# A graph convolution's message fetch by mask products on TensorE and one maximum on VectorE, and a bank per tile in the next block's opening

## The chip, the cores and the metric

One core of a Trainium2 chip runs the whole program. The metric is device time in microseconds (us) of one execution; lower is better. Engines are named as in the profile: PE (TensorE; PEld are its weight loads), DVE (VectorE), ACT (ScalarE), POOL (GpSimd), SP (SyncE, which only issues transfers here). "POOLq" and the like are an engine's sequencer.

## The reference

Four layers on 6250 nodes of 512 features follow each other; the change touches the first, a two-layer graph convolution over 100,000 edges (`src`, `dst`, sorted by `dst`) with hidden width H = 8:

```python
def _gcn_conv(x, W, b, src, dst, norm):
    h = x @ W
    msg = h[src] * norm[:, None]
    return jax.ops.segment_sum(msg, dst, num_segments=N) + b
h = _gcn_conv(x, W1, b1, src, dst, norm)        # 512 -> 8
h = relu(layernorm(h) * gamma + beta)
out = relu(_gcn_conv(h, W2, b2, src, dst, norm)) * size_factors   # 8 -> 512
x = x + out                                      # x here is the input of the layer norm before
x = x + ffn_bitlinear(_layernorm(x))             # weights quantised in groups of 128, 1408 wide
x = x + graph_mean(_layernorm(x)) ; x = x + switch_moe(_layernorm(x))
```

## The kernel before

The program has four blocks with a barrier between them. The nodes lie in NT = 49 tiles of 128, the edges in 784 chunks of 128.

**Block A** (until 188 us) makes the hidden features `hid` of all nodes, the degrees and the edge lists, and stores the source ids' low parts as `lo_rows` in device memory.

**Block B** (190 to 813 us) is the first convolution's sum over edges. Each edge needs the 8 values of its source node: `msg_b`, one chunk at a time. There are two ways to fetch a chunk. POOL gathers it by an indirect DMA (`gather_units`, L122; 464 chunks). Or PE, DVE and ACT fetch it without a gather: M = 80 groups g of 4 chunks. SP loads the low ids of the group (`low`), ACT turns them into masks (`far`, L1093, then `los`, L1099, two each: 128 low ids of the even and of the odd tiles of a pair), PE multiplies the masks with the node values kept in SBUF (`parts`; three bf16 parts, two halves: 6 products for each chunk, `products`, L1131), which leaves in PSUM for each edge the 8 values of each of HT = 25 tile pairs, and DVE picks the right pair: four multiplications by a compare with the edge's tile number (`masked`, L927) and one sum over 25 (L935), into `picked`. Beside this loop the same engines quantise the feed-forward weights: 22 "wide" pieces (DVE L882 to L899, PE transposes L1140, ACT copy L1078, DVE `wide_rest` L906), one every second group, and 4 "down" pieces (DVE L882 to L913, PE L1150, ACT L1086, DVE L919). `piece_at` says at which group a piece stands, and `back` how many groups later its next step comes. `split_picked` (L947 to L953) splits what was picked in three bf16 parts, in four groups of five.

After the loop come some 50 small steps (L991 to L1022), and then the 49 tiles: for each, DVE copies the messages of 20 chunks (`mstage`, L183) and builds a one-hot of 128x2560 (L184), PE multiplies them (L210) and DVE reduces the result (L1028). Two buffers alternate (`onehot`, `onehot_b`). A tile waits until its chunks have come (`msg_ready`), those of POOL included. In these inputs every tile takes one unit of 20 chunks and begins some 16 chunks after the one before.

**Block C** (from 814 us) is the second convolution and the feed-forward layer. Its messages `msg_c` are fetched in the same two ways, MC = 8 groups (32 chunks) by products and 752 by POOL. Its opening is serial: the products, then tiles 0 to 3 (`own_rows` L1562, the unit of `build_unit` L163 to L173, PE L219 to L229, ACT `aggT` L1452), then the layer of each (PE L1368, ACT L1462, DVE L1572), statistics, norm and transposes (PE L1375, ACT L1480, DVE L1607), and only then the first feed-forward products (L1386). All tiles of the opening use one PSUM bank, `pB`. The order is written in `groups`: `first` and `ahead` are tables of steps by place.

**Block D** (from some 2100 us) is the last two layers; the change doesn't touch it.

Of the kernel before, what the change touches and what calls it, by code (L numbers as in the profile page):

```python
# [4 lines left out]
F32 = mybir.dt.float32  # L5
# [37 lines left out]
M = 80  # L43
MB = 5
LR = 4
HT = -(-NT // 2)
assert 4 * M * P <= E and 4 * M % V == 0 and M % MB == 0 and 4 * MB == U
MC = 8
# [130 lines left out]
def build(nc, dve, b, c0, t, firsts, dstT, ids, onehot, msg, mstage, ready, msg_ready):  # L179
# [8 lines left out]
def build_units_beside(nc, dve, t, units_done, free, ended, ranges, firsts, dstT, ids, onehot, msg, mstage, ready, used, msg_ready):  # L188

    c0, units = tile_range(dve, ranges, t)  # L190
    with dve.Fori(0, units) as b:
        n = built(nc, dve, units_done)
        dve.wait_ge(used, nc.s_assert_within(dve.snap(free), 1, NT * (CU + 1) + 1, skip_runtime_bounds_check_because="units of the tiles, plus one"))
        build(nc, dve, b, c0, t, firsts, dstT, ids, onehot, msg, mstage, ready, msg_ready)
# [6 lines left out]
def sum_rows(nc, pe, t, units_done, ranges, mstage, identb, zerob, acc, onehot, ready, used):  # L201
# [3 lines left out]
    with pe.Fori(0, units):  # L205
# [3 lines left out]
        for k in range(U):  # L209
            last = nc.tensor.matmul(acc, onehot[:, k, :], mstage[:, k, :], start=False, stop=False)  # L210
# [25 lines left out]
def groups(loop, part):  # L236
# [56 lines left out]
    for steps in (first, ahead):  # L293
        for place in sorted(steps):
            run(steps[place], 0, 0)
# [34 lines left out]
def program(nc, x, src, dst, node_vec, W1, b1, gamma, beta, W2, b2, w_gate, w_up, w_down,  # L330
            alpha, Wg, bg, switch_w, switch_b, expert_w, expert_b, out):
    with ExitStack() as whole:
# [18 lines left out]
        def dram(name, shape, dt):  # L351
# [6 lines left out]
        lo_rows = dram("lo_rows", (C, P), BF16)  # L358
        lasts = dram("lasts", (1, NT), F32)
# [24 lines left out]
        early_hi = sb(convs, "early_hi", [P, 4 * MC], F32)  # L384
# [6 lines left out]
            "span var std degs degs_std span_ps spanr row_ps ranges lows numbers pool hid1 stored ".split())}  # L391
        x_in = [[sem(f"a_x_in{j}_{k}") for k in range(G)] for j in range(2)]
        with ExitStack() as ctx:
# [6 lines left out]
            low_b = sb(ctx, "low_b", [EP, EB * P], BF16)  # L400
            hi_f = sb(ctx, "hi_f", [EP, EB, P], F32)
# [43 lines left out]
            def _(sp):  # L445
# [29 lines left out]
                sp.wait_ge(s["ext_out"], 48)  # L475
# [27 lines left out]
            def _(dve):  # L503
# [84 lines left out]
                def low_ids():  # L588
                    own.step(nc.vector.tensor_single_scalar(hi_i[:], src_em[:], 2 * P - 1, ALU.bitwise_and))
                    own.step(nc.vector.tensor_copy(low_b[:], hi_i[:]))  # L590
                    dve.sem_inc(s["lows"], 1)

# [165 lines left out]
            "tail picked d_wq d_ps d_hi d_lo d_out ohs prod masked reduced parts far".split())}  # L758
        w_in = [sem(f"b_w_in{j}") for j in range(2)]
        wd_in = sem("b_wd_in")  # L760
        lo_in = [sem(f"b_lo_in{j}") for j in range(LR)]
        landed = [sem(f"b_landed{h}") for h in range(2)]
        with ExitStack() as ctx:
# [43 lines left out]
            def piece_at(g):  # L807
                if g < 4 * FB:
                    return ("wide", g // 2) if g % 2 == 0 else None
# [1745 lines left out]
```

## Time and profile before

| | us |
|---|---|
| runs of the kernel | 3475.45, 3487.32, 3489.5 |
| median | 3487.32 |
| span of the profiled execution (its own time; nothing else is listed with it) | 3485.4 |
| busy in it: PE, DVE, ACT, POOL | 2719.8, 2119.6, 1256.3, 2093.5 |

In the timelines below a row is one instruction or several alike, with start, duration, engine, line, operation, what is written and read, and in brackets how long the engine sat idle before it and what released it. Without brackets the row began as soon as the engine was free. "<-issue" is idle time in which the engine waited for no semaphore that the profile shows: its sequencer was at work.

### The profile page before, as it was taken

To read this page: it belongs to the slowest core of one execution; us is meant where nothing else is said; L and a number is where in the kernel's file an instruction comes from. 1 tells how busy PE (TensorE), PEld (TensorE's weight loads), DVE (VectorE), ACT (ScalarE), POOL (GpSimd) and SP (SyncE) were. 2 spreads that over 40 slices of the span, in tenths; PEclk is the share of its full clock that TensorE was granted. 3 is DMA by queue.
4 is the path that set the end of the run, shared out by engine and by line. 5 is a ranking of instruction groups with operands and counts; after the bars stand their busy time and mean duration, and the time that the engine had idled before them with its cause. 6 is when DMAs were issued, how large, how long until landed. Compare 5 with 4: busy or idle time off the path is not lost. (4 is left out here: it accounts for less than half of the span.)

```text
span 3485.4 us, 58362 instructions
## 1 busy us (share of the span) xinstructions
PE 2719.8 (78%) x15905; PEld 1951.7 (56%) x15906; DVE 2119.6 (61%) x4040; ACT 1256.3 (36%) x2029; POOL 2093.5 (60%) x2157
## 2 busy tenths in 40 slices
PE   6955557222799999999989995778787878878899
PEld 6945546122577777777777774333343433335687
DVE  8778888986466666666666655333444344443676
ACT  2444457002345444444444554001121212214444
POOL 0067777775777777777760002777777777772454
PEclk9667779556799999999999997999999999998899
DMA  3122233002133333333332324777777777775564
GB/s 100 61 60 48 48 81 80 5 5 54 29 105 98 98 100 94 95 95 103 91 104 94 104 100 157 215 227 232 231 240 232 244 235 246 236 240 170 175 213 128
DMA packets 237234, 459.23 MB, mean 132 GB/s; under 512 B 80060, under 2 KB 102828, under 8 KB 236994
## 3 DMA queue, kind: packets, MB, share of 16 engines
q0 software_dynamic: 111360, 235.84, 25.3%
q1 hardware_dynamic: 125634, 220.46, 19.1%
q8 instruction: 118, 1.93, 0.2%
q14 instruction: 122, 1.00, 0.1%
HBM read 389.41 MB, written 73.25 MB: 133 GB/s over the span
## 5 line engine op out<-in xcount | busy, mean ns | idle before, releaser
L122 POOL DMA_INDIRECT msg_c<-hid_rows,srcT x752 | 762.8, 1014 | 240.1 <-issue 224.9
L1868 POOL DMA_INDIRECT rows<-xn_rows,srcT x784 | 742.9, 948 | 268.6 <-issue 241.6
L2019 PE MATMUL pV<-rows,oh 128*128 x2240 | 554.4, 395 | 143.3 <-DVE oh L2332 59.0
L122 POOL DMA_INDIRECT msg_b<-hid_rows,srcT x464 | 453.5, 977 | 148.3 <-issue 135.8
L1386 PE MATMUL pGc<-xT,wgu_hi 128*128 128x384 f32 (+1 forms) x1848 | 476.7, 380 | 38.7 <-ACT gate_sum L1486 21.7
L2019 PEld LDWEIGHTS pV<-rows,oh 128*128 x2240 | 223.6, 100 | 459.9 <-issue 287.1
L1417 PE MATMUL acc<-wd,hT 128*128 128x512 f32 x1617 | 405.7, 398 | 18.0 <-DVE hT L1630 18.0
L1386 PEld LDWEIGHTS pGc<-xT,wgu_hi 128*128 128x128 f32 x1848 | 340.0, 192 | 105.8 <-issue 60.6
L1417 PEld LDWEIGHTS acc<-wd,hT 128*128 128x128 f32 x1617 | 302.9, 189 | 89.8 <-issue 29.7
L2332 DVE SCALAR_TENSOR_TENSOR oh<-ids,bases,dstT 128x896 f32 x160 | 184.2, 1151 | 225.0 <-issue 161.6
L2320 DVE TENSOR_TENSOR agg<-agg,pV x161 | 110.2, 685 | 321.6 <-PE pV L2019 320.7
L1131 PE MATMUL pG<-parts,los 128*128 128x200 bf16 x1920 | 222.4, 286 | 37.4 <-ACT los L1099 19.2
L1131 PEld LDWEIGHTS pG<-parts,los 128*128 128x128 bf16 x1920 | 202.1, 114 | 56.4 <-ACT los L1099 27.6
L2170 ACT ACTIVATE wg<-agg,invdeg 128x512 f32 (+1 forms) x49 | 35.3, 721 | 544.9 <-DVEq L111 544.9
L1851 POOL IOTA bases<- 128x49 f32 x1 | 0.2, 188 | 330.6 <-POOLq L349 330.6
L2047 PE MATMUL pW<-wgT,aT 128*128 128x512 f32 x392 | 183.2, 611 | 13.0 <-DVEq L2355 12.7
L2114 PE MATMUL pY<-weT,erT 128*128 128x512 f32 (+1 forms) x768 | 193.1, 400 | 0.0
L1620 DVE SCALAR_TENSOR_TENSOR up_sum<-pU,wscale,up_sum 128x512 f32<-128x512 f32 (+1 forms) x154 | 105.1, 682 | 127.7 <-ACT up_sum L1492 123.7
L1492 ACT ACTIVATE up_sum<-pGc,wscale 128x512 f32<-128x512 f32 (+1 forms) x154 | 97.7, 634 | 215.3 <-PE pGc L1386 215.2
L1614 DVE SCALAR_TENSOR_TENSOR gate_sum<-pGc,wscale,gate_sum 128x512 f32<-128x512 f32 (+1 forms) x154 | 105.4, 685 | 111.1 <-PE pGc L1386 76.3
L1386 PE MATMUL pGc<-xT,wgu_lo 128*128 128x512 f32 (+1 forms) x462 | 171.0, 370 | 0.0
L1386 PE MATMUL pU<-xT,wgu_hi 128*128 128x512 f32 (+1 forms) x616 | 165.2, 390 | 6.2 <-DVE up_sum L1620 6.2
(402 smaller groups left out, 4663.6 us busy)
## 6 DMA issues: line engine op xcount, KB each, us to landing
wd<-wd_rows SPq DMA_DIRECT2D x154, 512.0 KB
we<-in_L_ffn_expert_w SPq DMA_DIRECT2D x16, 1024.0 KB, 8.7
x_rows<-xr SPq DMA_DIRECT2D x49, 256.0 KB, 3.4
xn_rows<-pair SPq DMA_DIRECT2D x49, 256.0 KB, 2.0
rows<-xn_rows,srcT POOLq DMA_INDIRECT x784
res<-x_rows SPq DMA_DIRECT2D x49, 256.0 KB, 3.9
x_rows<-agg SPq DMA_DIRECT2D x49, 256.0 KB, 4.2
xt<-in_x SPq DMA_DIRECT2D x48, 256.0 KB, 2.8
```

The costliest lines, as they stand in the source:

```text
L122: nc.gpsimd.indirect_dma_start(msg[:, c, :], None, table, bass.IndirectOffsetOnAxis(ap=srcT[:, c:c + 1], axis=0)).then_inc(landed[u % 2], 16)
L1131: last = nc.tensor.matmul(into, los[:, g % 2, b, k * P:(k + 1) * P], parts[:, j, b].rearrange("p f h -> p (f h)"), start=(b == 0 and j == ...
L1386: last = nc.tensor.matmul(ps[:, 0:n], w, v, start=(m == 0), stop=(m == len(terms) - 1))
L1417: last = nc.tensor.matmul(acc4[j][:], h, wd[:, slot, w, :], start=(f == 0 and m == 0), stop=(f == FB - 1 and m == 2))
L1614: nc.vector.scalar_tensor_tensor(gate_sum[:, 0:n], pG[1][:, 0:n], wscale[:, f, 1:2], gate_sum[:, 0:n], ALU.mult, ALU.add).then_inc(s["gate ...
L1620: nc.vector.scalar_tensor_tensor(up_sum[:, 0:n], pU[0][:, 0:n], wscale[:, FB + f, 0:1], up_sum[:, 0:n], ALU.mult, ALU.add).then_inc(s["up_ ...
L1868: nc.gpsimd.indirect_dma_start(rows[:, u % RING, c, :], None, xn2_rows, bass.IndirectOffsetOnAxis(ap=srcT[:, u * Q + c:u * Q + c + 1], axi ...
L2019: last = nc.tensor.matmul(pV[:, ds(to, 1), :].rearrange("p a d -> p (a d)"), oh[:, ds(to, 1), c, :].rearrange("p a d -> p (a d)"), rows[:, ...
L2047: nc.tensor.matmul(pW[:], aT[:, k % 2, c, :], wgT[:, c, :], start=(c == 0), stop=False)
L2114: last = nc.tensor.matmul(pY[f % 2][0:n, :], erT[:, f % 2, j, c, 0:n], weT[:, e % 2, k, c, :], start=(j, k, c) == terms[0], stop=(j, k, c) ...
L2320: nc.vector.tensor_tensor(at, at, pV[:, ds((v + 1) % 2, 1), :].rearrange("p a b -> p (a b)"), ALU.add).then_inc(s["added"], 1)
L2332: nc.vector.scalar_tensor_tensor(oh[:, ds(v % 2, 1)].rearrange("p a q n -> p (a q) n"), bc(ids.unsqueeze(1), (P, Q, P)), bases[:, ds(tile, ...
```

## The change

In block B the number of groups goes from 80 to 110 (440 chunks), POOL gathers the other 344. A group's work is another. DVE makes the mask of the odd tiles by one compare (`odd`), ACT makes only the even one (`far`, `los`) and a new mask `beside` from the high ids: |tile pair of the edge - own partition| on 25 partitions. For each chunk PE first multiplies `beside` with `outside`, which holds -2^122 where the row is the column's tile pair, and adds the six products as before: a wrong pair gets a value near -2^122 or lower, the right one its own. DVE then takes one maximum over 25, straight from PSUM (`pick`). Three groups are under way instead of two (AHEAD), six loads instead of four (LB). A wide piece stands at every third group, a down piece at every tenth. Block A makes the high ids (`high_b`) and stores them (`hi_rows`). The tiles of block B build the one-hot in pairs of bf16 from small numbers (`rel`, `pairs`), as block C did already. `parts` is made by six copies with dense output instead of three with a strided one, and the eight steps for `hiT` are gone.

In block C the opening has MC = 10 groups in the new form, all low ids are loaded ahead of `node_vec` and `x`, tiles 0 to 3 have a bank each and an order of their own (`opening`).

```diff
-M = 80
+M = 110
+MW = 3
+MD = 10
+AHEAD = 3
-MC = 8
+MC = 10
@@ build (block B's tiles)
+    nc.vector.tensor_scalar(rel, dstT[:, at], firsts[:, ds(t, 1)], None, ALU.subtract).then_inc(related, 1)
     nc.vector.tensor_copy(mstage[:], msg[:, at, :])
-    nc.vector.scalar_tensor_tensor(onehot[:], bc(ids.unsqueeze(1), (P, U, P)), firsts[:, ds(t, 1)],
-                                   bc(dstT[:, at].unsqueeze(2), (P, U, P)), ALU.add, ALU.is_equal).then_inc(ready, 1)
+    dve.wait_ge(related, n + 1)
+    full = (P, U // 2, P, 2)
+    nc.vector.tensor_tensor(pairs, bc(numbers.unsqueeze(1), full), bc(rel.rearrange("p (g j) -> p g j", j=2).unsqueeze(2), full),
+                            ALU.is_equal).then_inc(ready, 1)
@@ groups
-    for steps in (first, ahead):
-        for place in sorted(steps):
-            run(steps[place], 0, 0)
+    opening = [(part.prepare, 0), (part.prepare, 1), (part.prepare, 2), (part.prepare, 3),
+               (part.build, 0), (part.sums, 0), (part.build, 1), (part.layer1, 0), (part.sums, 1), (part.build, 2), (part.layer1, 1),
+               (part.sums, 2), (part.build, 3), (part.layer1, 2), (part.sums, 3), (part.layer1, 3),
+               (part.stats, None), (part.scale, None), (part.norm, 0), (part.norm, 1),
+               (part.turn, 0), (part.norm, 2), (part.turn, 1), (part.norm, 3), (part.turn, 2), (part.turn, 3)]
+    run(opening, 0, 0)
@@ block B, DVE
-                def select(g):
+                def odd(g):
+                    dve.wait_ge(lo_in[g % LB], (g // LB + 1) * 16)
+                    if g >= AHEAD:
+                        dve.wait_ge(s["prod"], g - AHEAD + 1)
+                    nc.vector.tensor_scalar(los[:, g % AHEAD, 1, :], lo8[:, g % LB, :], lanes[:, 3:4], None, ALU.is_equal).then_inc(s["odds"], 1)
+
+                def pick(g):
                     dve.wait_ge(s["prod"], g + 1)
...
+                    nc.vector.tensor_reduce(picked[:, g // MB % 2, 4 * (g % MB):4 * (g % MB) + 4, :].rearrange("p (b c) f -> p b (c f)", b=2),
+                                            pG[g % AHEAD][:, :, 0:2 * H * HT].rearrange("p b (c h) -> p b c h", h=HT),
+                                            AX, ALU.max).then_inc(s["reduced"], 1)
@@ block B, ACT
+                    nc.scalar.activation(far[:], lo8[:, g % LB, :], ACT.Abs, bias=lanes[:, 0:1]).then_inc(s["far"], 1)
...
+                    nc.scalar.activation(beside[:, g % AHEAD, :], hi8[:, g % LB, :], ACT.Abs, bias=lanes[0:HT, 0:1]).then_inc(s["besides"], 1)
                     act.wait_ge(s["far"], g + 1)
...
+                    nc.scalar.activation(los[:, g % AHEAD, 0, :], far[:], ACT.Relu, bias=lanes[:, 2:3], scale=-1.0).then_inc(s["evens"], 1)
@@ block B, PE
+                    pe.wait_ge(s["besides"], g + 1)
+                    pe.wait_ge(s["evens"], g + 1)
+                    pe.wait_ge(s["odds"], g + 1)
+                    if g >= AHEAD:
+                        pe.wait_ge(s["reduced"], g - AHEAD + 1)
                     for k in range(4):
...
+                        nc.tensor.matmul(into, beside[:, g % AHEAD, k * P:(k + 1) * P], outside[:].rearrange("p f h -> p (f h)"), start=True, stop=False)
```

Three places show how the order of instructions changes. First DVE in block B's loop, at the first wide piece, before:

```order
L927 SCALAR_TENSOR_TENSOR masked<-iota,hiT,pG 128x200 x4
L935 TENSOR_REDUCE picked<-masked 128x32
L906 TENSOR_TENSOR wgu_lo<-pW,wgu_hi 128x256
L927 SCALAR_TENSOR_TENSOR masked<-iota,hiT,pG 128x200 x4
L935 TENSOR_REDUCE picked<-masked 128x32
L882 TENSOR_REDUCE sc<-wraw 128x4
```

and in the changed kernel, between two wide pieces:

```order
L969 TENSOR_REDUCE picked<-pG 128x32
L963 TENSOR_SCALAR los<-lo,lanes 128x512
L969 TENSOR_REDUCE picked<-pG 128x32
L963 TENSOR_SCALAR los<-lo,lanes 128x512
L943 TENSOR_TENSOR wgu_lo<-pW,wgu_hi 128x256
L969 TENSOR_REDUCE picked<-pG 128x32
L963 TENSOR_SCALAR los<-lo,lanes 128x512
L919 TENSOR_REDUCE sc<-wraw 128x4
```

Five DVE instructions a group became two, and `wide_rest` comes after the second group behind its piece instead of after the first. Second, DVE at one tile of block B (ISA, TENSOR_LOAD, REGISTER_ALU and branches are the sequencer's own instructions), before:

```order
L144 TENSOR_LOAD ranges
L144 ISA x2
L191 UNCONDITIONAL_BRANCH
L191 ISA
L181 ISA
L183 ISA
L183 COPY mstage_b<-msg_b 128x480
L184 ISA
L184 SCALAR_TENSOR_TENSOR onehot_b<-ids_b,firsts,dstT 128x2560
L195 ISA
L191 COMPARE_AND_BRANCH
```

and now:

```order
L151 TENSOR_LOAD ranges
L151 ISA x2
L201 UNCONDITIONAL_BRANCH
L201 ISA
L188 ISA
L190 ISA
L190 TENSOR_SCALAR rels<-dstT,firsts 128x20
L191 ISA
L191 COPY mstage_b<-msg_b 128x480
L192 REGISTER_ALU
L194 TENSOR_TENSOR onehot_b<-numbers_b,rels 128x2560
L205 ISA
```

The sequencer's work is all there still, with one instruction more on DVE. Third, PE behind block C's first tile; before, the next thing was tile 1's sums in the same bank:

```order
L229 MATMUL pB<-identb,zerob 32x128 x4
L144 TENSOR_LOAD ranges
L144 ISA x2
L219 MATMUL pB<-identb,own_rows 32x128
L219 MATMUL pB<-identb,zerob 32x128 x3
```

now the tile's layer comes first, and the next tile's sums go to another bank:

```order
L239 MATMUL pB<-identb,zerob 32x128 x4
L1439 MATMUL accs<-w2b,aggT 128x512
L151 TENSOR_LOAD ranges
L151 ISA x2
L229 MATMUL pU<-identb,own_rows 32x128
L229 MATMUL pU<-identb,zerob 32x128 x3
```

## Rows read from the trace of the kernel before

**Rows 1.** The gathers of blocks B and C, by line: duration min/median/max, first and last start

```profile
L122 POOL DMA_INDIRECT msg_c<-hid_rows,srcT x752: 938/944/2239, 815.1 to 1816.8; - x188
L122 POOL DMA_INDIRECT msg_b<-hid_rows,srcT x464: 938/944/1736, 191.2 to 791.8; - x155
```

**Rows 2.** Timeline of DVE at the end of block B

```profile
795.25 0.28 DVE L183 COPY mstage<-msg_b 128x480 bf16 x1 [7.70 <-POOLq L872]
...
799.16 0.18 DVE L1028 TENSOR_REDUCE agg<-pW 128x8 f32<-128x24 f32 x1 [0.75 <-PE pW L212]
```

**Rows 3.** Timeline of DVE in block B's loop, a wide piece and a down piece

```profile
204.22 0.99 DVE L935 TENSOR_REDUCE picked<-masked 128x32 f32<-128x800 f32 x1
205.12 0.68 DVE L882 TENSOR_REDUCE sc<-wraw 128x4 f32<-128x512 f32 x1
...
209.75 1.42 DVE L927 SCALAR_TENSOR_TENSOR masked<-iota,hiT,pG 128x200 f32<-128x200 f32 x4
...
492.68 1.61 DVE L882 TENSOR_REDUCE sc<-wdraw 128x11 f32<-128x1408 f32 x1
...
501.66 1.42 DVE L927 SCALAR_TENSOR_TENSOR masked<-iota,hiT,pG 128x200 f32<-128x200 f32 x4
```

**Rows 4.** Timeline of DVE at the loop's end and the first tiles

```profile
613.28 0.32 DVE L947 CAST msg_b<-picked 128x160 bf16<-128x160 f32 x1
...
628.29 0.34 DVE L183 COPY mstage<-msg_b 128x480 bf16 x1 [1.93 <-issue]
628.55 2.87 DVE L184 SCALAR_TENSOR_TENSOR onehot<-ids_b,firsts,dstT 128x2560 bf16<-128x2560 f32 x1
631.34 0.27 DVE L183 COPY mstage_b<-msg_b 128x480 bf16 x1
```

**Rows 5.** Groups of PE's products and of ACT's masks in block B

```profile
L1131 PE MATMUL pG<-parts,los 128*128 128x200 bf16 x1920 | 222.4, 286 | 37.4 <-ACT los L1099 19.2 <-DVEq L966 17.7
L1099 ACT ACTIVATE los<-far,lanes 128x512 bf16<-128x512 bf16 x160 | 106.7, 714 | 5.4 <-PE pG L1131 2.8
```

**Rows 6.** Timeline of PE in block B: the first groups, and late ones

```profile
198.54 7.04 PE L1131 MATMUL pG<-parts,los 128*128 128x200 bf16 x48 [17.74 <-DVEq L966]
209.78 1.11 PE L1140 MATMUL pW<-ident,wq 128*128 128x128 f32 x4 [4.20 <-DVE wq L899]
...
490.84 2.23 PE L1131 MATMUL pG<-parts,los 128*128 128x200 bf16 x24 [0.56 <-ACT los L1099]
```

**Rows 7.** Windows of block B's loop: us, busy of PE, PEld, DVE, ACT, POOL (x), PE clock, DMA share, GB/s

```profile
202.00:463.00 261.00, 152.97 (x1136) 137.14 (x1135) 211.78 (x516) 125.07 (x194) 198.17 (x202) 0.78 0.22 48
463.00:615.00 152.00, 93.41 (x900) 84.37 (x898) 135.03 (x258) 98.01 (x151) 114.89 (x115) 0.87 0.37 85
```

**Rows 8.** Timeline of ACT at the first masks of block B

```profile
193.09 1.33 ACT L1093 ACTIVATE far<-lo,lanes 128x512 bf16<-128x512 bf16 x2 [11.70 <-DMA lo<-lo_rows]
```

**Rows 9.** Timeline of DVE at the start of block B

```profile
190.11 5.97 DVE L957 COPY parts<-own 128x400 bf16<-128x400 bf16 x3 [1.78 <-PEq L349]
```

**Rows 10.** Timeline of DVE in block C's opening: two tiles, the last layer

```profile
856.07 1.49 DVE L173 TENSOR_TENSOR onehot<-numbers_c,rel_c 128x2560 bf16<-128x2560 bf16 x1
857.84 0.15 DVE L1564 TENSOR_SCALAR first_id<-first_id 128x1 f32<-128x1 f32 x1 [0.27 <-DVE onehot L173]
858.70 0.20 DVE L1562 COPY own_rows<-own 128x32 bf16<-128x32 bf16 x1 [0.70 <-DVE first_id L1564]
859.45 0.24 DVE L163 CAST mstage<-msg_c 128x160 bf16 x1 [0.56 <-issue]
...
885.74 0.75 DVE L1572 SCALAR_TENSOR_TENSOR xr<-xn,small,xr 128x512 f32<-128x512 f32 x1 [2.16 <-ACT xn L1462]
```

**Rows 11.** Timeline of DVE at tile 6 of block C

```profile
935.08 0.24 DVE L163 CAST mstage<-msg_c 128x160 bf16 x1 [6.98 <-POOLq L118]
```

**Rows 12.** Timeline of PE at the same place

```profile
938.11 0.72 PE L226 MATMUL pB<-onehot,mstage 128*24 128x128 bf16 x20 [3.23 <-DVE onehot L173]
```

**Rows 13.** Timeline of POOL: a gather at block C's first tile

```profile
856.35 2.04 POOL L122 DMA_INDIRECT msg_c<-hid_rows,srcT  x1 [0.30 <-DMA msg_c<-hid_rows,srcT]
```

More of the change, by code:

```diff
@@ L209, in sum_rows @@
         for k in range(U):
[L210 removed]
+            last = nc.tensor.matmul(acc, pairs[:, k // 2, :, k % 2], mstage[:, k, :], start=False, stop=False)
         last.then_inc(used, 1)
@@ L1021, in _ @@
                 own.step(nc.vector.tensor_copy(counts[:], v[5]))
-                own.step(nc.vector.tensor_copy(ids, iota[:]))
+                dve.wait_ge(s["numbers"], 2)
                 units_done, free, ended = (tally(dve, n) for n in ("units_done", "free", "ended"))
@@ L1096, in low @@
-                    if g >= 2:
-                        act.wait_ge(s["prod"], g - 1)
-                    for k in range(2):
-                        last = nc.scalar.activation(los[:, g % 2, k, :], far[:, k, :], ACT.Relu, bias=lanes[:, 2:3], scale=-1.0)
-                    last.then_inc(s["ohs"], 1)
-                act.wait_ge(s["lanes"], 2)
-                low(0)
-                low(1)
+                        act.wait_ge(s["evens"], g)
+                    nc.scalar.activation(far[:], lo8[:, g % LB, :], ACT.Abs, bias=lanes[:, 0:1]).then_inc(s["far"], 1)
@@ L1105, in _ @@
+                act.wait_ge(s["lanes"], 3)
+                for g in range(AHEAD):
+                    low(g)
                 for g in range(M):
-                    if g + 2 < M:
-                        low(g + 2)
-                    for back in (1, 0):
-                        kind, i = piece_at(g - back) or (None, 0) if g >= back else (None, 0)
+                    for back in (2, 1):
+                        kind, i = piece_at(g, back)
+                        if kind == "down" and back == 2:
+                            down(i, 2)
@@ L1297, in _ @@
                     load_x(0, k)
-                for g in range(LR, MC):
-                    low(g)
                 def gate(i, g, f):
@@ L1523, in _, with odd @@
                 own = Steps(dve, s["dve"])
+                for j in range(3):
+                    for k in range(2):
+                        last = nc.vector.tensor_copy(parts[:, j, k], own3[:, :, j * H:(j + 1) * H].rearrange("p (h k) f -> p k f h", k=2)[:, k])
+                own.step(last)
+                dve.sem_inc(s["parts"], 1)
+                def odd(g):
+                    dve.wait_ge(lo_in[g % LC], (g // LC + 1) * 16)
+                    if g >= AHEAD:
+                        dve.wait_ge(s["prod"], g - AHEAD + 1)
+                    nc.vector.tensor_scalar(los[:, g % AHEAD, 1, :], lo8[:, g % LC, :], lanes[:, 3:4], None, ALU.is_equal).then_inc(s["odds"], 1)
@@ L1543, in _ @@
-                for j in range(3):
-                    own.step(nc.vector.tensor_copy(parts[:, j].rearrange("p k f h -> p h k f"),
-                                                   own3[:, :, j * H:(j + 1) * H].rearrange("p (h k) f -> p h k f", k=2)))
-                dve.sem_inc(s["parts"], 1)
                 for g in range(MC):
-                    select(g)
+                    pick(g)
+                    if g + AHEAD < MC:
+                        odd(g + AHEAD)
                 dve.wait_ge(s["reduced"], MC)
```

324 lines of the change are left out of this document (181 added, 143 removed).

## The prediction

> **What bounds the kernel now.** The change touches blocks A, B and C only, so I read those and take the rest as a constant that moves with block C's end. The groups by line come first: POOL's gathers of block B run without a gap from 191.2 to 792.7 us [rows 1], 601.5 us for 464 chunks, 1.296 us each. The reader is to see that this is almost the whole of block B. Then the end of the block in DVE's timeline: the last tile's copy waits 7.70 us for POOL's sequencer, and the last reduction ends at 799.3 [rows 2]. The tiles themselves go 3.05 us apart (628.29 to 631.34, [rows 4]), so without POOL the 49th would begin at 628.3 + 48 x 3.05 = 775, not at 795.25. Block B thus has two chains of nearly one length: POOL's gathers, and the loop of 80 groups followed by 49 tiles; shortening one alone would give 20 us at most. The change touches both.
>
> Within the loop DVE is busy for 211.8 of 261 us in the stretch with the wide pieces and 135.0 of 152 after it, PE for 153.0 and 93.4 [rows 7]. DVE is the engine to count; PE is the one to watch.
>
> **POOL's chain.** 344 gathers instead of 464: 120 x 1.296 = 156 us less. Four small POOL instructions stand ahead of it now; I allow 2 us. It ends near 193 + 446 = 639 us. The tile that needs the last chunk comes 85 us later (below), so POOL leaves the path, and what it may lose is covered by those 85 us.
>
> **The loop.** Its start: ACT's first masks began at 193.09, two activations took 1.33 [rows 8], and one alone 0.71 [rows 5], so three with the wait between them end at 195.2. Before, DVE held PE until 198.54 [rows 6], with the three copies of `parts` (5.97 us, [rows 9]) and the `hiT` steps. Now there are six copies of half the size. Their reads are as strided as the writes were, so the bounds are 0.36 us each (one element a cycle) and 0.99 (as before); I take 0.4, and at the upper bound PE starts at 196 instead of 195. The first group's 28 products at 7.04 / 48 = 0.147 us each [rows 6] take 4.1, so the first pick starts at 199.3 instead of 202.8.
>
> The pick reduces 1600 elements from PSUM. The sum over 800 took 0.99 us and its successor began 0.90 later [rows 3]; by that row's slope (0.83 for 800) the pick is 1.82, and 1.73 to its successor. It takes the place of four products and a sum, 2.4 us. The odd mask is 512 bf16 elements with one scalar. No row shows it. From below: the dense bf16 copy of 480 elements took 0.27 us [rows 4], with a successor 0.2 later. From above: one element a cycle as in the 800-element row, 0.53 + 0.16 = 0.69. I take 0.2 to the successor, since the copy is nearest in type and layout; the upper end goes to a rival.
>
> The Trainium skill, VectorE: DVE Perf Modes, section on the perf-mode tier table, gives bf16 `tensor_scalar` in SBUF four times the plain rate and any reduction the plain rate; its 693 ns for 2048 elements would make 0.29 us here, and the sum would be the same.
>
> A wide piece occupies DVE 4.63 us (205.12 to 209.75, [rows 3]) and its rest 0.4; a down piece 8.98 (492.68 to 501.66) and its rest 1.8. A step of `split_picked` takes 0.3. So three groups with a wide piece: 3 x 1.93 + 2.4 x 0.3 + 5.03 = 11.5 us, 22 times: 254. The other 44 groups: 44 x 1.93 + 35 x 0.3 + 4 x 10.8 = 139. I add 3 us for the last ten groups, where PE (28 x 2.23 / 24 = 2.60 us a group at full clock, [rows 6]) is slower than DVE's 2.2. The loop's last pick ends at 199 + 254 + 139 + 3 = 595 against 613.3. ACT needs 3 x 0.7 = 2.1 us a group and is hidden behind either. PE needs for three groups 84 products and 4 transposes. At full clock that is 7.8 + 1.1 = 8.9 us of 11.5; at the mean of before, 222.4 / 1920 = 0.116 us [rows 5], it is 10.8. Both fit, the second with 7% to spare. Three groups are under way, so a pick has its product ready some 9 us before its turn, and the order of the rows is kept by DVE. PE queues its transposes ahead of the next group, and ACT its copy ahead of the next masks; both cost PE idle time but not DVE's.
>
> **From the loop to the tiles** it took 613.28 to 628.29 [rows 4], 15.0; the copy to `ids` (0.3) is gone: first tile at 610 us.
>
> **The tiles.** DVE's own work for one falls from 2.87 + 0.27 + 0.17 to a subtraction (0.25), a copy, the pair form (1.49, [rows 10]) and the reduction, some 1.95 us with overlaps. But the sequencer's work stays: loading the range, entering the loop, computing addresses. Block C shows it uncovered: 0.71 us from `first_id` to `own_rows` (the load) and 0.75 to `mstage` (the loop entry) [rows 10]; the first tile's 1.93 [rows 4] is the same two with a few register moves. With the loop's tail and the reduction's issue, some 0.5, the next subtraction comes 2.0 us after the pair form starts, and the pair form 0.4 after that: 2.4 us a tile. The bounds are 1.95 (all hidden) and 3.05 (no gain). 48 x 2.4 = 115, and 3.0 for the last one to the end of its reduction: 610 + 115 + 3 = 728, against 799.3: **-71 us**. By parts: 18 from the loop, 33 from the tiles, 20 from POOL's wait.
>
> **Block A** has two more DVE steps of 0.6 us, early, where DVE runs histograms ahead of PE, and one more store on SP: 0.
>
> **Block C's opening.** Products: PE can start 2 us earlier (`parts` dense) and its ten groups take 4.1 + 9 x 2.6 = 27.5 us without the stall for late low ids, so the first build comes some 3 us earlier in spite of two groups more. Then from tile 1's `mstage` (859.45) to the end of tile 3's layer (886.5, [rows 10]) it took 27.0 us: three builds, then four layers one after the other, each waiting 2.16 us for ACT. Interleaved, a layer costs DVE its 0.75 and its chain runs under the next build: two builds and two layers at 5.6 us, a last build of 3 and its chain of 5, about 19. That is 8 us. The four transposes in their own banks overlap: 4 us. Sum 15. But the supply comes in: tile 6 waited 6.98 us for POOL already and PE 3.23 behind it [rows 11, 12]. Its chunks are 88 gathers of before, 80 now. At (935.1 - 815.1 - 1.7) / 88 = 1.344 us each, the 80th lands at 816 + 107.5 + 1.7 = 925 (block C's old clock), 10 us earlier. So the start of the group is 15 us earlier and tile 6 only 10: **-10 us**.
>
> At the first tile a gather took 2.04 us instead of 0.94 while the pair one-hot ran [rows 13]; 0.94 is the median [rows 1]. [...] Worked out from the rows: 110 odd masks of 0.3 us push POOL's end from 639 to 672, under the 725 of the last tile, and ten of them push tile 6 of block C by 3 us. That is a case of its own, at -78.
>
> **Sum:** -71 - 10 = -81 us. The profiled span is 3485.4 and becomes 3404; the median, 1.9 above the span, becomes **3406**.
>
> **Rivals.** (1) The tiles keep 3.05 us, the sequencer being the bound: 48 x 0.65 = 31 less, 3437. For it: 1.93 us of issue at one tile. Against: the tail isn't 0.9 us longer in any row. (2) The odd mask goes one element a cycle: 110 x 0.4 = 44 us, 3450. Against it is the copy's row. (3) PE partly slow. After 4 to 5 us of idling PE's transposes and the products behind them ran slow: the granted clock of the stretch was 0.78 [rows 7]. If it stays so with shorter gaps, PE delays some picks, 10 to 25 us: 3416 to 3431. (4) The slower side: PE's products go at 0.147 us all along, as in the first groups, near the lower level of its clock (1.2 of 2.4 GHz). Then three groups take 84 x 0.147 + 1.1 = 13.4 us (+41 over 22), the other 44 take 44 x 4.12 + 10 = 191 (+49): +90 in all, 3496, and at 0.163 us some 3530. It decides from 0.143 us a product. Against it: PE would then have no idle time, and rows without a gap ran at 0.093. (5) The change gives more: tiles at 2.0 us and an opening that isn't held by tile 6: 3382.
>
> **Numbers.** Forecast, the port's case in it, 3394 to 3420: 0.50. Rival 1: 0.13; 2: 0.10; 3: 0.14; 4: 0.05; 5: 0.08. The range 3388 to 3450 takes in rivals 1 to 3 and leaves out 4 and most of 5. A measurement of this kernel can tell about 0.5% (17 us) from no change: faster 0.93, within 0.5% 0.04, slower 0.03, from rival 4's two ends and mishaps not thought of.
>
> **What the profile after would show.** Picks of 1.82 us; odd masks under 0.3; a wide piece every 11.5 us with no idle time of DVE in front of a pick; the first tile at 610; tiles 2.4 us apart with 0.4 to 0.5 of "issue" in front of the subtraction; no wait for POOL in block B, whose gathers end near 640; block B's last reduction at 728; in block C's first 130 us a wait of some 12 us for POOL at tile 6. I am wrong if DVE waits for PE in the loop by more than a few us, if the pick isn't 1.8, or if the tile phase is no shorter than 140 us.

## The result, and the profile after: slower, where faster was forecast

| | before | after |
|---|---|---|
| median of the runs timed together, us | 3488.41 | 3520.69 |
| span of the profiled execution | 3485.4 | 3521.7 |
| start of the first and the last pick of block B's loop | 204.2, 612.3 | 202.2, 709.3 |
| block B's last reduction ends | 799.3 | 849.9 |
| from there to block D's first gather | 1350.5 | 1336.2 |

The ratio is 1.0114 (95% 1.0082 to 1.0145; of the two medians alone 1.009): about 1% slower, where 3406 us was forecast. The span grew by 36.3 us: block B's last reduction is 50.6 later, block C 14.3 shorter, the rest, 1335.6 us from block D's first gather to the end, the same. So everything is lost in block B, and the tiles are not the place (125.7 us from the first tile to the end of the last reduction; 118 was forecast). It is the loop. Its last pick was to end at 595 us and ends at 710.3.

The same windows as [rows 7], of the changed kernel (busy us of PE, PEld, DVE, ACT and POOL, PE clock):

```profile
202.00:463.00 261.00, 215.05 (x1585) 141.74 (x1584) 159.76 (x367) 111.05 (x176) 196.95 (x202) 0.85 0.28 58
463.00:615.00 152.00, 130.54 (x979) 86.28 (x980) 86.12 (x164) 74.08 (x116) 114.06 (x116) 0.87 0.32 72
```

DVE, which the forecast took for the bound, is busy for 160 of 261 us instead of 212. PE is at 215. PE is the busiest engine now, and even so it stands still in between. Two things in PE's timeline tell why. First, products without a gap at full clock; the forecast had priced them by the last row of [rows 6]:

```profile
643.84 0.26 PE L1163 MATMUL pG<-outside,beside 25*128 25x200 bf16 x1
644.02 0.69 PE L1166 MATMUL pG<-parts,los 128*128 128x200 bf16 x6
644.65 0.25 PE L1163 MATMUL pG<-outside,beside 25*128 25x200 bf16 x1
```

The seven products of a chunk take 644.65 - 643.84 = 0.81 us, a group 3.23. The six of `parts` start 0.088 us apart (0.69 less the last one's 0.25, over five). So the mask product takes the rest: 0.81 - 6 x 0.088 = 0.28 us. The forecast gave it 0.093. Second, PE, ACT and DVE at a wide piece:

```profile
343.38 0.69 PE L1166 MATMUL pG<-parts,los 128*128 128x200 bf16 x6
343.90 0.60 PE L1175 MATMUL pW<-ident,wq 128*128 128x128 f32 x4
347.06 0.32 PE L1163 MATMUL pG<-outside,beside 25*128 25x200 bf16 x1 [2.56 <-ACT beside L1130]
347.32 1.18 PE L1166 MATMUL pG<-parts,los 128*128 128x200 bf16 x6
348.43 0.34 PE L1163 MATMUL pG<-outside,beside 25*128 25x200 bf16 x1
```

```profile
344.54 0.59 ACT L1112 CAST wgu_hi<-pW 128x512 fp32r<-128x512 f32 x1 [5.96 <-PE pW L1175]
345.02 0.72 ACT L1126 ACTIVATE far<-lo,lanes 128x512 bf16<-128x512 bf16 x1
345.64 0.70 ACT L1130 ACTIVATE beside<-hi,lanes 25x512 bf16<-25x512 bf16 x1
346.26 0.71 ACT L1132 ACTIVATE los<-far,lanes 128x512 bf16<-128x512 bf16 x1
```

```profile
340.87 0.99 DVE L969 TENSOR_REDUCE picked<-pG 128x32 f32<-128x800 f32 x1 [0.52 <-PE pG L1166]
341.78 0.34 DVE L963 TENSOR_SCALAR los<-lo,lanes 128x512 bf16<-128x512 bf16 x1
345.16 0.42 DVE L943 TENSOR_TENSOR wgu_lo<-pW,wgu_hi 128x256 fp32r<-128x256 f32 x1 [3.04 <-ACT wgu_hi L1112]
345.50 0.98 DVE L969 TENSOR_REDUCE picked<-pG 128x32 f32<-128x800 f32 x1
```

Read across the three: ACT had nothing to do for 5.96 us, because its next instruction was the copy of the piece, which waits for PE's transposes. These stand behind the groups that PE had queued. When they end at 344.5, ACT copies and only then makes the masks of the next group, and PE has stopped. Every wide piece makes a closed chain of PE, ACT and PE again: the same stop of 2.56 us stands at each of the 22. Behind it the products go at half speed (seven in 348.43 - 347.06 = 1.37 us). The granted clock is 0.50 there, PE's lower level of 1.2 GHz:

```profile
347.00:352.00 5.00, 4.94 (x26) 3.08 (x27) 4.04 (x11) 3.89 (x6) 3.78 (x5) 0.50 0.09 8
```

A wide cycle takes 14.43 us (the first and the 67th pick are 317.4 us apart, over 22), where 11.5 was forecast.

Of the 18 runs behind this text eleven (k128, nomask, actorder, m80, m80_again, m80_c, m80_d, oldopen, oldopen_c, oldtile, oldtile_c) fell into a state in which the engines stood still for 60 to 90 us at a time at many places and the kernel before took 5364 to 5412 us, so of these only durations between such stops are used.

### The profile page after: what moved, and what is told of

The parts are those of the page before. It is cut to its first block and busy times, and to the rows that moved or that the text cites. A ratio compares the mean times of both kernels' runs of the same rounds, so it can differ in the third digit from the quotient of the medians.

```text
span 3521.7 us, 61189 instructions
## 1 busy us (share of the span) xinstructions
PE 2916.8 (83%) x17153; PEld 2016.6 (57%) x17154; DVE 1996.1 (57%) x3913; ACT 1257.3 (36%) x2037; POOL 1972.0 (56%) x2036
## 5 line engine op out<-in xcount | busy, mean ns | idle before, releaser
L1459 PE MATMUL gates<-xT,wgu_hi 128*128 128x384 f32 (+1 forms) x1848 | 475.2, 379 | 38.4 <-ACT gate_sum L1557 20.5
L1490 PE MATMUL accs<-wd,hT 128*128 128x512 f32 x1617 | 407.3, 399 | 16.1 <-DVE hT L1705 16.1
L129 POOL DMA_INDIRECT msg_b<-hid_rows,srcT x344 | 340.2, 989 | 114.0 <-issue 106.3
L1459 PEld LDWEIGHTS gates<-xT,wgu_hi 128*128 128x128 f32 x1848 | 337.6, 191 | 106.0 <-issue 61.3
L1490 PEld LDWEIGHTS accs<-wd,hT 128*128 128x128 f32 x1617 | 304.5, 190 | 88.3 <-issue 27.9
L1166 PE MATMUL pG<-parts,los 128*128 128x200 bf16 x2640 | 354.2, 279 | 0.0
L1163 PE MATMUL pG<-outside,beside 25*128 25x200 bf16 x440 | 120.6, 274 | 91.4 <-ACT beside L1130 66.1
L969 DVE TENSOR_REDUCE picked<-pG 128x32 f32<-128x800 f32 x110 | 108.6, 988 | 127.4 <-PE pG L1166 126.9
L1563 ACT ACTIVATE up_sum<-gates,wscale 128x512 f32<-128x512 f32 (+1 forms) x154 | 97.7, 634 | 216.2 <-PE gates L1459 216.1
L1459 PE MATMUL gates<-xT,wgu_lo 128*128 128x512 f32 (+1 forms) x462 | 171.3, 371 | 0.0
```

What stands on the lines that cost most here:

```text
L129: nc.gpsimd.indirect_dma_start(msg[:, c, :], None, table, bass.IndirectOffsetOnAxis(ap=srcT[:, c:c + 1], axis=0)).then_inc(landed[u % 2], 16)
L969: nc.vector.tensor_reduce(picked[:, g // MB % 2, 4 * (g % MB):4 * (g % MB) + 4, :].rearrange("p (b c) f -> p b (c f)", b=2), pG[g % AHEAD] ...
L1163: nc.tensor.matmul(into, beside[:, g % AHEAD, k * P:(k + 1) * P], outside[:].rearrange("p f h -> p (f h)"), start=True, stop=False)
L1166: last = nc.tensor.matmul(into, los[:, g % AHEAD, b, k * P:(k + 1) * P], parts[:, j, b].rearrange("p f h -> p (f h)"), start=False, stop=( ...
L1459: last = nc.tensor.matmul(ps[:, 0:n], w, v, start=(m == 0), stop=(m == len(terms) - 1))
L1490: last = nc.tensor.matmul(acc4[j][:], h, wd[:, slot, w, :], start=(f == 0 and m == 0), stop=(f == FB - 1 and m == 2))
```

## The experiments

**k128, nomask, actorder, m80.** k128: `beside`, `outside` and the loaded `hi8` of block B 128 partitions tall, zeros in `outside` from row 25 on.

```diff
-            outside = sb(ctx, "outside", [HT, H, HT], BF16)
+            outside = sb(ctx, "outside", [P, H, HT], BF16)
```

> The changed kernel with the mask product of block B on 128 rows of weights instead of 25 (the 103 rows more of outside are zero, beside is 128 partitions tall; same result). In the changed kernel a chunk's seven products take 0.81 us, six of them 0.088 each, so the mask product takes 0.28: 0.18 until it starts, 0.19 until the next one does. Theory A: the switch between weights of 25 and of 128 rows is what costs, so seven take 0.62, a group 2.5 instead of 3.23 us and the loop 110 x 0.75 = 80 us less if PE is its bound, less where ACT or DVE become it: 3440 to 3465. Rival B: the cost lies with the start of an accumulation or another moving tile, a group stays at 3.2 us and the time at 3520.

nomask leaves the mask product of block B out, so that the maximum runs over the wrong tile pairs too:

```diff
-                        nc.tensor.matmul(into, beside[:, g % AHEAD, k * P:(k + 1) * P], outside[:].rearrange("p f h -> p (f h)"), start=True, stop=False)
...
-                                                        start=False, stop=(b == 1 and j == 2))
+                                                        start=(b == 0 and j == 0), stop=(b == 1 and j == 2))
```

> The changed kernel without the mask product in block B (so the maximum runs over wrong values and the messages are wrong; ACT still makes the mask beside, and PE waits for it). 24 products a group. If the mask product costs 0.28 us, a group falls from 3.23 to 2.1 us on PE and DVE and ACT become the bound of the loop: the gap between groups without a piece near 2.2 to 2.4 us, the loop 80 to 110 us shorter, 3410 to 3440. If it costs only the 0.093 of the forecast, a group falls to 2.86 and the loop by some 40 us: 3480. The stops of PE at the wide pieces (2.56 us behind the transposes) stay in both.

actorder:

```diff
                 for g in range(M):
+                    if g + AHEAD < M:
+                        low(g + AHEAD)
                     for back in (2, 1):
...
-                    if g + AHEAD < M:
-                        low(g + AHEAD)
```

> The changed kernel with one edit on ACT in block B's loop: the masks of the group three ahead stand before the copies of the pieces instead of behind them. In the changed kernel PE idles 2.56 us behind every wide piece's transposes, because ACT waits for these, copies (0.59), and makes three masks only then. Theory A: these stops go, 22 x 2.56 = 56 us and some 10 at the down pieces, and the loop is PE's alone: three groups and four transposes in 9.7 + 0.6 = 10.3 us instead of 14.9, where part of the difference is also PE's lower clock after the stops: 3425 to 3465. Rival B: the copy now comes 2 us later, DVE's rest of the piece and the next pick with it, and PE waits for the pick instead: 3500 to 3520.

m80:

```diff
-M = 110
+M = 80
-MW = 3
+MW = 2
-MD = 10
+MD = 4
```

> The changed kernel with 80 groups by products in block B instead of 110 (a wide piece every second group, a down piece every fourth), POOL gathering 464 chunks as before. Theory A (with 28 products at 3.23 us a group and a stop of PE at every piece, each group more than 80 costs more on the loop than it takes off POOL's chain): 30 groups less take 30 x 3.23 = 97 us out of the loop, whose last pick comes near 610 instead of 710, but POOL's gathers end near 793 again and block B near 800 instead of 850. The rest of the program stays as in the changed kernel (it was 14 us shorter than before there). 3472 to 3480 us, so about 12 us faster than the kernel before. Rival (the loss isn't in the number of groups but behind it, in tiles or block C): block B ends no earlier than 840, 3515 or more.

The times (5237, 5194, 5197 and 5385 us, the kernel before 5367.5) can't be set against the expectations. The distances of picks can. Late groups without a piece: 2.40 us in k128, 2.06 in nomask, 3.23 in actorder and m80. So 28 products of one height take 28 x 0.086, 24 take 24 x 0.086, and the 25-row form costs 0.83 us a group more. A wide cycle took 10.1 us in actorder, in k128 some 11.3. Whether m80 was worth anything these distances don't say; m80_e below does.

**order, rows**: the two edits each alone. order is actorder's edit. rows is k128 without its larger loads: `beside` is tall but loaded and written on 25 rows only, the others are zeroed once.

```diff
-                    nc.scalar.activation(beside[:, g % AHEAD, :], hi8[:, g % LB, :], ACT.Abs, bias=lanes[0:HT, 0:1]).then_inc(s["besides"], 1)
+                    nc.scalar.activation(beside[0:HT, g % AHEAD, :], hi8[:, g % LB, :], ACT.Abs, bias=lanes[0:HT, 0:1]).then_inc(s["besides"], 1)
...
+                nc.gpsimd.memset(beside[:], 0.0).then_inc(s["lanes"], 1)
```

> The changed kernel with one edit on ACT in block B's loop: the masks of the group three ahead stand before the copies of the pieces instead of behind them. Nothing else. In the changed kernel a wide cycle of three groups takes about 14.35 us and the ten groups of a down piece 42.5, with 2.56 us in each in which PE waits for beside behind its transposes. Theory A: the order alone makes a wide cycle 10.1 us, at which DVE sets it, and a down piece's ten groups 34.8: 22 x 4.25 + 4 x 7.7 = 124 us off the loop. The last pick comes near 585, block B ends near 725, the whole is 3396 us where the kernel before takes 3488 (ratio 0.974), although a group still takes 3.23 us of PE. Rival B (the mask product's price is the main cause): the loop gains no more than the visible stops, 26 x 2.56 = 67 us, ratio 0.990.

> The changed kernel with the mask product of block B on 128 rows of weights: beside is 128 partitions tall, its rows from 25 on are zeroed once by POOL and never written again, so SP loads no more than before; ACT's order stays. Theory A: a group without a piece takes 2.4 us instead of 3.23 (ACT's three masks are its bound then), a wide cycle some 11.3 instead of 14.35 and a down piece's ten groups 37.8 instead of 42.5: 22 x 3.05 + 4 x 4.7 + 3 = 89 us off the loop, 3432 us where the kernel before takes 3488 (ratio 0.984). The stops of PE for beside behind the transposes stay, about 1.9 to 2.6 us each. Rival B (the order of ACT is the main cause): ratio 1.000 or more, the wide cycle stays at 13.5 us or more.

order: 3395.5 us against 3490.4, ratio 0.9735 (0.9702 to 0.9767); last pick at 574.7, last reduction at 716.3. Theory A had 3396, and its rival 0.990: moving two lines on ACT takes 125 us off the changed kernel. PE at a wide piece, without the stop:

```profile
302.16 0.69 PE L1166 MATMUL pG<-parts,los 128*128 128x200 bf16 x6
302.69 0.60 PE L1175 MATMUL pW<-ident,wq 128*128 128x128 f32 x4
303.22 0.25 PE L1163 MATMUL pG<-outside,beside 25*128 25x200 bf16 x1
```

Windows of its loop, wide pieces and the rest, columns as above:

```profile
202.00:425.00 223.00, 223.00 (x1937) 154.18 (x1936) 191.06 (x444) 135.96 (x216) 169.00 (x173) 1.00 0.35 77
425.00:575.00 150.00, 144.87 (x1249) 98.95 (x1248) 102.64 (x165) 88.97 (x139) 113.52 (x110) 1.00 0.41 97
```

PE is busy for 223 of 223 us and granted its full clock. A wide cycle takes 10.18 us, three groups at 3.23 and the transposes. Of the 4.25 us that a cycle lost by the order, 2.56 are the stop that the trace names; the other 1.7 come with it, the products at the lower clock behind the stop.

rows: 3420.3 us, ratio 0.9805 (0.9770 to 0.9839), a little better than expected (0.984); last pick at 605.1. PE at a down piece, and 6 us later at full clock:

```profile
471.31 0.32 PE L1164 MATMUL pG<-outside,beside 128*128 128x200 bf16 x1 [2.45 <-ACT beside L1131]
...
477.17 0.25 PE L1164 MATMUL pG<-outside,beside 128*128 128x200 bf16 x1
477.25 0.68 PE L1167 MATMUL pG<-parts,los 128*128 128x200 bf16 x6
477.77 0.25 PE L1164 MATMUL pG<-outside,beside 128*128 128x200 bf16 x1
```

Seven products in 0.60 us instead of 0.81, with the same 0.25 us for each; what went is the distance to the neighbours (from the start of a mask product to the next start 0.18 us, from the start before it 0.19; they became 0.08 and 0.09). The stops of 2.45 to 2.56 us behind a piece stay, and a wide cycle is 11.07 us. The Trainium skill, TensorEngine Tiling (Array Packing), section Key Properties, has the array drain when the tiling mode changes. A cost at both changes of height in every chunk, as measured here, would fit that; but which mode the 25-row products ran in, no run shows, so this cause of the cost stays open.

**both**: order's and k128's edits together.

> The changed kernel with two edits in block B: the mask product on 128 rows of weights (a group without a piece took 2.40 us with it instead of 3.23) and ACT's masks ahead of the pieces' copies (a wide cycle of three groups took 10.1 us with it instead of 14.5). Theory A, both causes are apart and add up: PE then needs 84 x 0.088 + 0.6 = 8.0 us a wide cycle and DVE's own work (4.63 + 0.4 + 3 x 1.4 + steps of the split) sets it at 10.1, groups without a piece 2.4. Loop: 22 x 10.1 + 40 x 2.4 + 4 x 8.5 = 352 us, last pick near 555; first tile 14 later at 569, 48 x 2.56 = 123, last reduction at 695 against 799 before; POOL's gathers end at 648. With block C's opening 14 us shorter the whole is 104 + 14 = 118 less than the kernel before: ratio 0.966, 3370 us where that takes 3488. Rival B: the wide cycle stays longer than 11 us, or tile 6 of block C, waiting for POOL's gathers, takes the 14 us back: ratio 0.974 or more.

3366.5 us against 3489.6, ratio 0.9656 (0.9617 to 0.9694), as expected in the sum but not in its parts. A wide cycle takes 9.06 us (10.1 expected), the last pick stands at 530.1 (555), the first tile at 545.7. But two tiles at the end wait 10.5 and 7.0 us for POOL, and the last reduction is at 687.6 (695). POOL's 344 gathers end only at 682, where 648 was expected.

**tiles**: the kernel before with the new tile form in block B alone.

```diff
-    nc.vector.scalar_tensor_tensor(onehot[:], bc(ids.unsqueeze(1), (P, U, P)), firsts[:, ds(t, 1)],
-                                   bc(dstT[:, at].unsqueeze(2), (P, U, P)), ALU.add, ALU.is_equal).then_inc(ready, 1)
+    nc.vector.tensor_tensor(pairs, bc(numbers.unsqueeze(1), full), bc(rel.rearrange("p (g j) -> p g j", j=2).unsqueeze(2), full),
+                            ALU.is_equal).then_inc(ready, 1)
```

> The kernel before with block B's tiles alone as in the changed one: rel and a pair form of the one-hot (1.49 us) instead of the form of 2.87 us. The groups, the masks and block C stay. Theory A, from the forecast: block B hangs on POOL's gathers at its end, so a shorter tile brings nothing, ratio 0.998 to 1.002. Rival B: POOL's gathers are slower beside the pair form. With the two edits above together (the tile phase then ran beside POOL's gathers), POOL started 30 gathers in 50 us of that phase, 1.67 us each, and 39 in 50 us in the kernel before. Then 49 tiles at some 0.6 us each add 27 to 50 us to POOL's chain and block B ends near 830 instead of 799: ratio 1.008 to 1.014.

3531.6 us, ratio 1.0131 (1.0097 to 1.0165), as rival B had it: the part of the change that the forecast counted at -33 us makes the kernel before slower by itself. Block B's last reduction is at 829.6, 30.3 late, though its gathers began 7 us earlier (184.2): POOL's 464 gathers take 640 us instead of 601.5, which is 38.5 more. Seven of the tiles wait for POOL, up to 20 us. (Another 8 us lie in block D, which isn't touched; its length from the first to the last gather was 1010 to 1018 us in the runs, and what sets it stays open.) POOL's and DVE's timeline in the tile phase:

```profile
700.88 2.10 POOL L122 DMA_INDIRECT msg_b<-hid_rows,srcT  x1 [0.30 <-issue]
703.28 0.94 POOL L122 DMA_INDIRECT msg_b<-hid_rows,srcT  x1 [0.30 <-issue]
704.53 1.38 POOL L122 DMA_INDIRECT msg_b<-hid_rows,srcT  x1 [0.31 <-issue]
706.22 2.12 POOL L122 DMA_INDIRECT msg_b<-hid_rows,srcT  x1 [0.30 <-issue]
```

```profile
700.67 1.49 DVE L187 TENSOR_TENSOR onehot<-numbers_b,rels 128x2560 bf16<-128x2560 bf16 x1
...
703.61 1.49 DVE L187 TENSOR_TENSOR onehot_b<-numbers_b,rels 128x2560 bf16<-128x2560 bf16 x1
...
706.03 1.49 DVE L187 TENSOR_TENSOR onehot<-numbers_b,rels 128x2560 bf16<-128x2560 bf16 x1
```

A gather that starts inside a one-hot (at 700.88, 704.53 and 706.22) ends 0.8 us after the one-hot has ended; the one at 703.28, which starts ahead of one, takes its 0.94.

**best**: order and rows in block B, the tall `beside` in block C too, and 12 groups there.

> The changed kernel with ACT's order of the first kernel, the tall zeroed beside in blocks B and C, and 12 groups by products in block C instead of 10. With both edits of block B (and loads 128 partitions tall) the kernel took 3366.5 us, its tiles waited 10.5 and 7.0 us for POOL at the end, and the last reduction came at 687.6. With the loads back at 25 partitions POOL gains 8 gathers until the tiles begin, 10 us: last reduction near 677. Block C: a group 2.5 instead of 3.23 us (12 groups take no longer than 10 did), 8 gathers less ahead of tile 6, which waited 5.06 us for them: 5 us. In all 15 less, 3351 us, ratio 0.961. If POOL's waits come from its own slower gathers alone and not from the loads: 3362, ratio 0.964.

3358.0 us, ratio 0.9623 (0.9588 to 0.9657): the fastest here, 132 us under the kernel before. The first guess on POOL fell: with small loads its gathers end at 681, one microsecond earlier than in both, the last reduction stands at 686.5 and not at 677, and 29 or 30 gathers start in each 50 us of the tile phase in both kernels. So it isn't the loads; tiles had pointed to the tile form.

**oldtile_e**: best with the old form of the one-hot in block B, but with its ids from `iota` in SBUF, where the kernel before had a copy in PSUM (the changed kernel has no bank left for them). Its first two runs, oldtile and oldtile_c, gave only the 3.08 us of a tile.

```diff
+    nc.vector.scalar_tensor_tensor(pairs[:], bc(numbers.unsqueeze(1), (P, U, P)), firsts[:, ds(t, 1)],
+                                   bc(dstT[:, at].unsqueeze(2), (P, U, P)), ALU.add, ALU.is_equal).then_inc(ready, 1)
...
+                    build_units_beside(nc, dve, t, units_done, free, ended, ranges, firsts, dstT, iota[:], rels[:, j, :], onehots[j], msg, mstages[j],
```

> The kernel best with block B's one-hot in the old form (no rel; ids read from SBUF). Theory A: 38 or 39 gathers start in 50 us of the tile phase instead of 30, POOL ends near 648 instead of 680, no tile waits for it: last reduction at 546 + 48 x 3.08 + 4 = 698 instead of 686, about 3369 us, ratio 0.9655 where best had 0.9623. Rival B: POOL ends near 680 again and makes the last tiles wait.

3418.6 us, ratio 0.9807 (0.9766 to 0.9849), so 60 us slower than best, against theory A and worse than rival B: POOL's gathers end at 722 and not near 680. (The profile is of the fastest of its five runs, 3396.8 us; from the first gather to the last reduction block B takes 547.5 us in it, 57.5 more than in best.) A window of POOL's gathers in the tile phase (busy, clock, DMA share, GB/s), and both engines:

```profile
550.00:600.00 50.00, 45.01 (x17) 0.50 0.04 2
```

```profile
602.46 2.77 POOL L129 DMA_INDIRECT msg_b<-hid_rows,srcT  x1 [0.30 <-issue]
605.53 2.78 POOL L129 DMA_INDIRECT msg_b<-hid_rows,srcT  x1 [0.30 <-issue]
```

```profile
601.53 2.87 DVE L191 SCALAR_TENSOR_TENSOR onehot_b<-iota,firsts,dstT 128x2560 bf16<-128x2560 f32 x1
604.61 2.87 DVE L191 SCALAR_TENSOR_TENSOR onehot<-iota,firsts,dstT 128x2560 bf16<-128x2560 f32 x1
```

One gather for each one-hot, in step with it. The kernel before, where the same instruction has the same length but reads `ids` from PSUM [rows 4], had 40 gathers in 50 us (starts from 650 to 700) and 0.94 us for each beside its one-hots:

```profile
650.12 2.87 DVE L184 SCALAR_TENSOR_TENSOR onehot_b<-ids_b,firsts,dstT 128x2560 bf16<-128x2560 f32 x1
```

```profile
650.40 0.94 POOL L122 DMA_INDIRECT msg_b<-hid_rows,srcT  x1 [0.30 <-issue]
651.65 0.94 POOL L122 DMA_INDIRECT msg_b<-hid_rows,srcT  x1 [0.30 <-issue]
```

So it isn't the pair form as such that holds POOL. What the two forms that hold it have in common, and the one that doesn't hold it lacks, is that DVE reads two tensors from SBUF; no run moved that one input alone, everything else being equal. The Trainium skill, SBUF — State Buffer, section "Who interferes with whom", says this of DVE instructions with two SBUF inputs and GpSimd instructions that read SBUF. The trace agrees (2.78 us a gather against 0.94), though not with the page's remark in brackets, marked there as inferred, that `tensor_tensor` leaves descriptor generation alone: a gather beside the pair form took up to 2.12 us.

**m80_e**: m80 again. By then tiles was known.

> The changed kernel with 80 groups in block B. Theory A: POOL is block B's bound again and is slowed by the pair form from the first tile (near 628) on: last reduction at 829 to 834 against 799, about +20 us on the kernel before in all, ratio 1.004 to 1.008. Rival B (POOL's gathers as in the kernel before): last reduction near 800, ratio 0.996.

3521.6 us, ratio 1.0092 (1.0060 to 1.0125): with 80 groups the kernel is as slow as with 110. The last pick comes at 604.1, 105 us earlier, and the last reduction at 836.3, 14 earlier: the last six tiles wait for POOL, whose 464 gathers end at 831. The 14 us don't reach the end: from there to block D's first gather it takes 7.7 us longer than in the changed kernel, and block D 9.4, though neither is touched; why stays open. This is the first line of DVE's waits from 620 to 840 us (five waits; the sixth, of 9.5 us, is at the last tile):

```profile
DVE rels L190 <- POOLq L125: 85.3, 5, 20.4
```

My first expectation for m80 (3472 to 3480) is refuted, and with it the guess that the number of groups is much of the loss: block B ends 50.6 us late with 110 groups, by the loop, and 37.0 late with 80, by POOL.

**oldopen**: best with block C's opening in its old order. Both its runs have stops inside the opening, so it stays open what the new order alone is worth.

> The kernel called best with the opening of block C in the order of before (all builds, then all layers, the norms and turns as the tables say); the banks per tile, the 12 groups and all of block B stay. Theory A: from tile 1 to the end of tile 3's layer it takes 8 us longer (the forecast's 27 against 19), tile 6 then waits 2 us less for POOL: +6, 3364 us, ratio to best 1.002. Rival B: POOL's supply of tile 6 sets block C's opening, so the order brings nothing and the two are within 2 us. Rival C: the old order, in which a layer waits for ACT each time, costs the whole 15 us of the forecast: 3373.

## Why the prediction was wrong, step by step

**The step that failed: "both cost PE idle time but not DVE's".** The forecast saw that PE's transposes and ACT's copy stand ahead of the next group and its masks, and priced this at nothing because three groups are under way and DVE was taken for the bound. order is the test, and it gives back 125 us. Three groups under way are no cover here: ACT can't make the masks of the group three ahead before PE's transposes have ended, and these stand behind every group whose masks are ready, so at their end PE has nothing left to do. The price was 4.25 us a wide cycle, 93 us in 22, and some 10 us in each down piece's ten groups (42.5 to 47.8 against 34 to 35). Nor does the step need PE as the bound to fail: with the cheap products of rows the stops stay, and a wide cycle takes 11.07 us against 9.06 in both, which has the other order.

**The premise under it: "28 x 2.23 / 24 = 2.60 us a group".** It took 3.23: a product of another height was priced like its neighbours. In the changed kernel the two causes overlap: rows alone takes 104 us off the loop, order alone 134.5, both together 179.

**A miscount that hid both.** The pick was taken for 1600 elements; it reads 4 x 200 = 800 from each partition and takes 0.99 us, as the row with 800 said. With 0.99 DVE's wide cycle is not 11.5 but 11.5 - 3 x 0.83 = 9.0 us, which is what best takes (9.06), and PE's own sum (7.8 + 1.1 = 8.9) would have stood beside it as a bound. The miscount made the pick too dear where the products had been taken too cheap, and the two nearly cancel: order, with PE at 3.23 and no stops, gives 3395, inside 3394 to 3420. Without the failed step the forecast would have come true by luck.

**The rivals.** Rival 4 named PE as the slower side from 0.143 us a product on, at a low clock all along. In the window with the wide pieces PE was busy for 215.05 us with 1585 matmuls, 0.136 each, and at full clock it is 3.23 / 28 = 0.115; what decided were the dearer mask product and the stops. So 3496 to 3530 held the result for a reason that wasn't its own, and "slower" had a chance of 0.03. Rival 3's mechanism, slow products behind idle time, did occur, but at 1.7 of the 4.25 us of a wide cycle (37 us in 22) it was larger than its 10 to 25 and came with stops that rival 3 didn't have. Rival 1 (3.05 us a tile), rival 2 (odd masks of 0.69) and rival 5 (tiles of 2.0) didn't occur.

**The tiles: "2.4 us a tile".** They run 2.41 and 2.70 us in turn, 2.56 on average: the idle time ahead of the subtraction is the 0.50 of issue that was forecast at one tile and 0.8 ("<-PE pW") at the next. Right in kind, 8 us off in all. In the changed kernel POOL ended at 649, ahead of the first tile (724), so the price on POOL stayed hidden. The step "what it may lose is covered by those 85 us" held for a loop as short as the one forecast: in order the tiles begin at 590.4, POOL ends at 669.9, and no tile waits for it. It doesn't hold for a shorter one: in best they begin at 545.7, and the last two wait 16 us in all.

**Smaller terms.** POOL's chain ended at 649 (639 forecast), so of the case that the odd masks hold its gathers up to 672 (the port's case) at most 10 of 33 us came: the gather of 2.04 us in [rows 13] stood beside a pair one-hot, which reads two tensors, and `odd` reads one. The odd mask took 0.34 us, 0.26 to its successor (0.2 forecast). From the end of the last pick to the first tile it was 14.0 us (15). The first pick came at 202.2 and not at 199.3: the six copies of `parts` took 3.82 us, 0.64 each and not 0.4, and the first products ran at half speed, seven in 1.37 us.

**Block C: -10**, measured -14.3, and its parts are off on both sides. Counted from block B's last reduction, the first tile's `own_rows` comes 7.4 us later (62.0 against 54.6) and not 3 earlier: PE starts 1.9 us earlier, but its ten groups take 37.6 us and not 27.5, the first at half speed and the late ones 3.23 us apart. From tile 1's `mstage` to the end of tile 3's layer it takes 16.2 us instead of 27.0, more than the 8 us forecast, and the turns overlap for the 4 us forecast. So tile 4's `own_rows` came 8 us earlier and not 15. Tile 6 then waited 3.57 us for POOL and not 12:

```profile
974.30 0.24 DVE L170 CAST mstage<-msg_c 128x160 bf16 x1 [3.57 <-POOLq L125]
```

## What to carry to other kernels

When a change moves work from one engine to another, ask first what stands ahead of that work in the queue of each engine that feeds it: an order of instructions can close a cycle (PE, ACT, PE) that no sum of busy times shows. Put what feeds the bound ahead of what the bound feeds; here two lines were worth 125 us. Price an operation of another shape by a row of that shape or by bounds, never by its neighbours, and check a gain that is hidden on one chain against the case in which the other chain has become short: the tile form that looked free lengthens POOL's gathers by 38 us when POOL is the bound.

## What the runs showed of the hardware that was not expected

- Products on 25 rows of weights between products on 128: each takes the same 0.25 us, but six and one take 0.81 us instead of 0.60 (rows). With zero rows up to 128 a product is no slower (0.25 us) and the 0.21 us are gone.
- A DVE instruction with two SBUF inputs holds POOL's indirect gathers until it ends, in the bf16 form of 1.49 us (30 gathers in 50 us) and in the float form of 2.87 (17 in 50 us, 2.78 us each). With one input in PSUM, the same 2.87 us instruction lets 40 start. Whether the pair form with its numbers in PSUM would be as fast and leave POOL alone was not tried.
- The masks by `tensor_scalar` (one tensor input, 0.34 us) in the loop hold POOL little: 344 gathers at 1.32 us each against 1.30.
